# Segment softmax of a graph layer on one core: node maxima by scans of the sorted edges, exponentials per edge, sums with a bf16 one-hot

## The chip, the cores and the metric

One core of a Trainium2 chip runs the whole layer in one launch. The metric is the device time of that core in microseconds; lower is better. Three undisturbed runs of the kernel before took 2481.23, 2489.24 and 2489.09 us, median 2489.09 us.

## The reference

A graph attention layer over N = 12500 nodes with D = 64 features and E = 212500 edges that are sorted by target node (`dst`).

```python
h_trans = features @ Watt_w.T + Watt_b
e_raw = jnp.sum(h_trans[dst] * jnp.tanh(h_trans[src] + e_r), axis=-1, keepdims=True)
e_ij = leaky_relu(e_raw / 8)
max_score = segment_max(e_ij, dst, num_segments=N)
exp_e = jnp.exp(e_ij - max_score[dst])
denom = segment_sum(exp_e, dst, num_segments=N)
alpha = exp_e / (denom[dst] + 1e-09)
h_neigh = segment_sum(features[src] * alpha, dst, num_segments=N)
h_out = leaky_relu((features + h_neigh) @ W1_w.T + W1_b + ((features * h_neigh) @ W2_w.T + W2_b))
return layernorm(features + h_out)
```

## The kernel before

The nodes are cut into 98 **blocks** of 128. Since the edges are sorted, the edges of a block lie in one window of 19 tiles of 128 edges, and a step works on such a window. 16 tiles are laid out with 16 consecutive edges to a partition (MAIN), the last 3 (TAIL) with one edge of a tile to a partition. The tiles of a block are handled in five **chunks** of 4, 4, 4, 4 and 3.

A setup of some 60 us projects all nodes (h_trans) and writes a table in HBM with a node's projection and its features, 128 numbers to a row. Then each block passes through these stages:

- **Gathers.** GpSimd (POOL) issues one indirect DMA for each tile, 128 rows of 512 bytes into `got` (L528). 17 are always issued, the last two only where the window has edges there; there are 1716 in all. `got` has four buffers, so a gather may run up to four blocks ahead.
- **One-hot.** VectorE (DVE) builds `other` = (node of the block differs from the edge's target), 128x2432 in bf16 (L1055). TensorE (PE) transposes its 19 tiles (L778), ScalarE (ACT) turns them over into `hotT` (L624).
- **Scores.** PE spreads the target's projection to the edges with `hotT` in three bf16 parts (L793, 57 matmuls of 64 columns). DVE adds the gathered projection to the edge's attributes (L1066), ACT takes tanh (L630), DVE multiplies and sums (L1077, one instruction pair for each tile).
- **Maxima.** `finish_scores` on DVE splits the scores in three bf16 parts (six chained small instructions), PE transposes them (L801), ACT copies (L647), PE adds for each tile a mask matmul and a selection matmul (L813, L814), which lay all the block's scores out node by edge. DVE takes their maxima (L1098), splits the maximum in three parts (`split_max`, six chained small instructions), PE spreads it back to the edges (L821), DVE subtracts (L1117, L1119).
- **Weights.** ACT computes for each tile the whole 128x128 matrix of exp(mask + score - max) in float32 (L641, 19 of them).
- **Sums.** PE multiplies that float32 matrix with the gathered features and a column of ones (L833, 19 matmuls of 65 columns, which the trace records as two each).
- **Node part.** DVE divides (`neighbours`), PE transposes and multiplies with W1 and W2 (L839, L844), DVE adds, and takes the norm's statistics (`residual`).

The order on each engine is written out by hand in `step(third, before, prev, b, nxt, ahead)`. In one step block b is scored, b-1 (`prev`) gets its maxima, b-2 (`before`) its weights, sums and division, b-3 (`third`) its node part, and the one-hot of b+1 (`nxt`) is made; SyncE (SP) loads the edges of b and the indices of b+2. Each engine runs its list in order, and semaphores count blocks. Four steps stand ahead of a loop of 23 turns of four steps; two steps and a hand-written ending follow it. At the end, when 93 blocks have their statistics, DVE inverts the deviations (L1154), POOL normalises those blocks in four large instructions (L348, L350), and SP stores them; DVE normalises the last ones.

## Time and profile before

| what | value |
|---|---|
| median of the runs | 2489.09 us |
| span of the profiled execution | 3764.5 us |
| TensorE clock granted, mean of the span | 0.509 |
| busy PE / DVE / ACT / POOL in the span | 2446.1 / 1444.2 / 1070.6 / 1834.0 us |
| instructions PE / DVE / ACT / POOL | 17304 / 7626 / 3100 / 1744 |
| largest group | L528, the gathers on POOL: 1716 of 1047 ns |
| chain that ended last | another core or an unknown queue 33%, PE 31%, issue 16%, DVE 14%, ACT 4% |

The profiled execution took half as long again as the undisturbed runs, and it is the only one of which single instructions are known. So durations of instructions are read from it, while its waits have to be judged one by one. A matmul's end is modelled; how fast matmuls follow each other is read from their starts. "remote" is idle time for which the trace names no instruction as releaser. In the timeline a row gives start, duration, engine, line, operation, and in brackets the idle time ahead of it and what ended it.

### The profile page before, as it was taken

To read this page: it belongs to the slowest core of one execution; us is meant where nothing else is said; L and a number is where in the kernel's file an instruction comes from. 1 tells how busy PE (TensorE), PEld (TensorE's weight loads), DVE (VectorE), ACT (ScalarE), POOL (GpSimd) and SP (SyncE) were. 2 spreads that over 40 slices of the span, in tenths; PEclk is the share of its full clock that TensorE was granted. 3 is DMA by queue.
4 is the path that set the end of the run, shared out by engine and by line. 5 is a ranking of instruction groups with operands and counts; after the bars stand their busy time and mean duration, and the time that the engine had idled before them with its cause. 6 is when DMAs were issued, how large, how long until landed. Compare 5 with 4: busy or idle time off the path is not lost.

```text
span 3764.5 us, 55969 instructions
## 1 busy us (share of the span) xinstructions
PE 2446.1 (65%) x17304; PEld 1825.6 (48%) x17304; DVE 1444.2 (38%) x7626; ACT 1070.6 (28%) x3100; POOL 1834.0 (49%) x1744
## 2 busy tenths in 40 slices
PE   3367676767666666666676766667675757676666
PEld 2245454545454444545454545545454545455445
DVE  4234333333333333433343333434333433334335
ACT  3122222222323232323222232323222222223233
POOL 4554454545454545454544545454545444454542
PEclk7555555555555555555555555555555555555555
DMA  6111212121111121111112111111212111211111
GB/s 152 48 51 48 52 45 52 45 51 47 49 48 49 47 49 48 49 49 49 49 49 52 45 49 47 49 48 48 55 44 53 44 51 46 51 47 49 47 48 35
DMA packets 254023, 191.31 MB, mean 51 GB/s; under 512 B 201156, under 2 KB 213656, under 8 KB 253880
## 3 DMA queue, kind: packets, MB, share of 16 engines
q0 software_dynamic: 55072, 113.24, 11.5%
q1 hardware_dynamic: 198808, 76.77, 8.7%
q14 instruction: 128, 1.05, 0.1%
q8 instruction: 15, 0.25, 0.0%
HBM read 180.27 MB, written 9.60 MB: 50 GB/s over the span
## 4 chain that ended last, share of the span: by engine, by line
another core or an unknown queue 33%; PE 31%; issue 16%; DVE 14%; ACT 4%; SPq 1%; DMA 0%; POOL 0%; DVEq 0%; POOLq 0%
PE ps_sc L814 10%; PE ps_sc L813 9%; PE ps_acc L833 7%; DVE edge L1077 3%; ACT hotT L624 3%; PE ps_hd L793 2%; DVE chunk_max L1098 2%; PE ps_other L778 1%; DVE edge L1066 1%; PE ps_acc L844 1%; PE ps_acc L801 1%; DVE score L1092 1%; DVE score L1090 1%; DVE rest L1089 1%
## 5 line engine op out<-in xcount | busy, mean ns | idle before, releaser
L528 POOL DMA_INDIRECT got<-table,src_i x1716 | 1796.4, 1047 | 1821.1 <-issue 1800.6
L833 PE MATMUL ps_acc<-got,weight 128*128 128x65 f32 x3724 | 895.2, 422 | 4.3 <-issue 3.6
L778 PE MATMUL ps_other<-ident,other 128*128 128x128 bf16 x1862 | 289.6, 305 | 862.4 <-issue 627.7
L833 PEld LDWEIGHTS ps_acc<-got,weight 128*128 128x128 f32 x3724 | 828.2, 329 | 27.0 <-issue 3.1
L624 ACT ACTIVATE hotT<-ps_other 128x512 bf16<-128x512 bf16 (+1 forms) x490 | 274.2, 576 | 1395.1 <-remote 1232.7
L778 PEld LDWEIGHTS ps_other<-ident,other 128*128 128x128 bf16 x1862 | 186.0, 139 | 959.5 <-issue 687.4
L1098 DVE TENSOR_REDUCE chunk_max<-ps_sc 128x1 f32<-128x512 f32 (+1 forms) x490 | 325.9, 665 | 678.3 <-PE ps_sc L814 550.7
L641 ACT ACTIVATE weight<-other,arg 128x128 f32<-128x128 bf16 x1862 | 580.6, 387 | 8.4 <-DVE arg L1119 8.2
L793 PE MATMUL ps_hd<-h,hotT 128*128 (+1 forms) x5586 | 439.6, 240 | 196.7 <-issue 194.9
L813 PE MATMUL ps_sc<-mask,other 128*128 128x128 bf16 x1862 | 541.5, 291 | 26.9 <-ACT score3T L647 26.9
L814 PE MATMUL ps_sc<-score3T,sel 57*128 57x128 bf16 x1862 | 530.6, 285 | 0.0
L630 ACT ACTIVATE edge<-edge 128x256 f32<-128x256 f32 (+1 forms) x490 | 198.0, 404 | 1096.2 <-DVE edge L1066 1066.9
L1077 DVE CUSTOM_DVE_ANT_0 edge<-edge,ps_hd 128x64 f32<-128x64 f32 x1862 | 298.0, 216 | 501.1 <-remote 489.3
L793 PEld LDWEIGHTS ps_hd<-h,hotT 128*128 128x128 bf16 x5586 | 360.4, 131 | 258.9 <-issue 236.2
L813 PEld LDWEIGHTS ps_sc<-mask,other 128*128 128x128 bf16 x1862 | 226.1, 121 | 209.8 <-ACT score3T L647 27.6
L814 PEld LDWEIGHTS ps_sc<-score3T,sel 57*128 57x128 bf16 x1862 | 189.0, 101 | 233.9 <-issue 38.0
L1117 DVE TENSOR_REDUCE edge_max<-ps_misc 128x19 f32<-128x57 f32 x98 | 21.2, 217 | 717.5 <-remote 714.7
L1066 DVE TENSOR_TENSOR edge<-edge,got 128x256 f32<-128x256 f32 (+1 forms) x490 | 199.8, 408 | 9.7 <-DMA got<-table,src_i 7.6
L801 PE MATMUL ps_acc<-ident,score 128*57 128x128 bf16 x98 | 27.3, 279 | 195.0 <-DVE score L1092 170.9
L1077 DVE DVE_READ_ACCUMULATOR2_ANT raw<- 128x1 f32 x1862 | 153.9, 83 | 0.0
L1055 DVE TENSOR_TENSOR other<-iota_h,dst_rel 128x2432 bf16<-128x2432 bf16 x98 | 139.7, 1425 | 3.4
L801 PEld LDWEIGHTS ps_acc<-ident,score 128*57 128x57 bf16 x98 | 12.2, 125 | 207.8 <-issue 207.8
(116 smaller groups left out, 1061.1 us busy)
## 6 DMA issues: line engine op xcount, KB each, us to landing
edge<-in_edge_attr SPq DMA_DIRECT2D x98, 512.0 KB
got<-table,src_i POOLq DMA_INDIRECT x1716
edge<-in_edge_attr SPq DMA_DIRECT2D x98, 96.0 KB
table<-hx SPq DMA_DIRECT2D x12, 512.0 KB
got<-in_x SPq DMA_DIRECT2D x3, 768.0 KB, 14.3
src_i<-in_src SPq DMA_DIRECT2D x98, 8.0 KB
src_i<-in_src SPq DMA_DIRECT2D x98, 1.5 KB
dst_i<-in_dst SPq DMA_DIRECT2D x98, 8.0 KB
```

The source lines that it names most:

```text
L528: pool.indirect_dma_start(got[b.four][:, g, 0:2 * D], None, table, bass.IndirectOffsetOnAxis(ap=src_i[b.four][:, g:g + 1], axis=0), bounds ...
L624: act.activation(hotT[b.four][:, a:z, :], ps, ACT.Copy, bias=1.0, scale=-1.0)\
L630: act.activation(edge[b.two][:, a:z, :], edge[b.two][:, a:z, :], ACT.Tanh).then_inc(tanh_done[c], 1)
L641: last = act.activation(weight[:, g, :], other[b.four][:, g, :], ACT.Exp, bias=arg[b.two][:, g:g + 1], scale=-MASKED)
L778: last = pe.transpose(ps_other[(b.two + c) % 2][:, k * P:(k + 1) * P], other[b.four][:, g, :], ident16[:, :])
L793: last = pe.matmul(ps_hd[(b.two + c) % 2][:, k * D:(k + 1) * D], hotT[b.four][:, g, :], rhs, start=(part == 0), stop=(part == 2))
L813: pe.matmul(spread, other[b.four][:, g, :], mask16[:, :], start=True, stop=False)
L814: last = pe.matmul(spread, sel[:, g, :], score3T[:, :], start=False, stop=True)
L833: last = pe.matmul(a_sum, weight[:, g, :], got[b.four][:, g, D:2 * D + 1], start=(g == 0), stop=(g == TILES - 1))
L1066: dve.tensor_tensor(edge[b.two][:, a:z, :], edge[b.two][:, a:z, :], got[b.four][:, a:z, 0:D], ALU.add).then_inc(added[c], 1)
L1077: last = dve.tensor_tensor_reduce(out=edge[b.two][:, g, :], in0=edge[b.two][:, g, :], in1=ps_hd[(b.two + c) % 2][:, k * D:(k + 1) * D], sc ...
L1098: dve.tensor_reduce(chunk_max[:, c:c + 1], ps_sc[(b.two + c) % 2][:, 0:(z - a) * P], AX.X, ALU.max)\
```

## The change

- **Layout.** MAIN becomes 17 tiles and TAIL 2, still 19.
- **One-hot.** DVE builds `hot` (equal, not differing) in five chunks (L1074). PE transposes it and ACT copies it in three **pieces** of 8, 8 and 3 tiles. `hotT` has two buffers in place of four.
- **Maxima.** The split of the scores, their transposition and spreading, the maxima over node rows, the split and spreading of the maximum all go. In place of them: two scans on DVE along each partition's 17 edges, forwards and backwards, in which the difference of neighbouring target numbers times 2^100 resets the running maximum (`gap`); the first and last value of each partition and the two tail tiles are laid in one row of 512 on one partition by four PE transposes (`lay_rows`); two scans along this row (`scan_row`); four small PE transposes back (`lay_back`); and three instructions that combine (`exponents`). ACT prepares the target numbers (`set_ids`, five instructions), DVE their differences (`set_gaps`), SP loads the row of target numbers (`load_row`, two more DMAs).
- **Weights.** One exponential of 128x19 on ACT.
- **Sums.** DVE multiplies the gathered features with the weights (`weight_rows`, `rows`), ACT and DVE split them in turns in three bf16 parts (`split`, `rest`, into `triple`), and PE takes 19 bf16 matmuls of 195 columns with `hot`. DVE adds the three parts (L1163). All this is done one step earlier than before: the weights belong to `prev`. 
- **Ending.** The loop's step also serves for the ends. The large normalisation on POOL now starts after the last block's node part.

```diff
             def gather(third, before, prev, b, nxt, ahead):
-                    pool.wait_ge(summed[0], b.n - (BUFS - 1))
+                    pool.wait_ge(weighted[0], b.n - (BUFS - 1))
...
+            def weigh(b):
+                act.wait_ge(arg_done, b.n + 1)
+                act.activation(weight[:, :], arg[:, :], ACT.Exp).then_inc(weights_done, 1)
...
+            def lay_back(b):
+                for k in range(2):
+                    pe.transpose(m_back[:, k:k + 1], row_max[0:1, k:2 * P:2], ident[0:1, 0:1])
+                for k in range(TAIL):
+                    last = pe.transpose(m_back[:, 2 + k:3 + k], row_max[0:1, (2 + k) * P:(3 + k) * P], ident[0:1, 0:1])
...
+            def sum_edges(b, p):
+                pe.wait_ge(parts_done[p], b.n + 1)
+                for g in range(*piece(p)):
+                    last = pe.matmul(a_sum, hot[b.four][:, g, :], triple[:, g, 0:SUMS],
+                                     start=(g == 0), stop=(g == TILES - 1))
...
+                chain("fwd", dve.tensor_tensor_scan(run_max[:, :], gap[:, 0:MAIN], score[:, 0:MAIN], LOWEST,
+                                                    ALU.add, ALU.max), b)
+                ends = MAIN - 1
+                dve.tensor_tensor_scan(part_max[:, ends::-1], gap[:, MAIN:0:-1], run_max[:, ends::-1], LOWEST,
+                                       ALU.add, ALU.max).then_inc(runs_done, 1)
+            def scan_row(b):
+                dve.wait_ge(rows_ps, b.n + 1)
+                chain("row", dve.tensor_tensor_scan(row_max[:, :], row_gap[:, 0:ROW], ps_row[0:1, 0:ROW], LOWEST,
+                                                    ALU.add, ALU.max), b)
+                dve.tensor_tensor_scan(row_max[:, ROW - 1::-1], row_gap[:, ROW:0:-1], row_max[:, ROW - 1::-1], LOWEST,
+                                       ALU.add, ALU.max).then_inc(row_done, 1)
...
+            def weight_rows(b, p):
+                dve.tensor_tensor(rows[:, a:z, :], got[b.four][:, a:z, D:2 * D + 1],
+                                  weight[:, a:z].rearrange("p (g d) -> p g d", d=1).to_broadcast([P, z - a, D + 1]),
+                                  ALU.mult).then_inc(weighted[p], 1)
+            def rest(b, k, p):
+                    dve.tensor_tensor(rows[:, a:z, :], rows[:, a:z, :], parts[:, a:z, 0, :], ALU.subtract)\
...
+                    dve.tensor_tensor(parts[:, a:z, 2, :], rows[:, a:z, :], parts[:, a:z, 1, :], ALU.subtract)\
```

What stands on DVE in the middle of a step of the kernel before, from the second chunk of scores to the weights' arguments, in the last steps ahead of the loop:

```order
L1098 TENSOR_REDUCE chunk_max<-ps_sc0 128x1
L1104 TENSOR_REDUCE node_max<-chunk_max 128x1
L1105 CAST max3<-node_max 128x1
L1106 TENSOR_TENSOR mrest1<-node_max,max3 128x1
L1107 CAST max3<-mrest1 128x1
L1108 TENSOR_TENSOR mrest2<-mrest1,max3 128x1
L1109 CAST max3<-mrest2 128x1
L1050 TENSOR_SCALAR dst_rel<-dst_i0,base 128x38
L1053 TENSOR_SCALAR base<-base 128x1
L1055 TENSOR_TENSOR other0<-iota_h,dst_rel 128x2432
L1077 ISA edge1,raw1<-edge1,ps_hd1 128x64
```

And on DVE in a step of the changed kernel, in the loop, from the row scans to the first remainder:

```order
L1116 SCALAR_TENSOR_TENSOR row_max<-row_gap,ps_row 1x512
L1118 SCALAR_TENSOR_TENSOR row_max<-row_gap,row_max 1x512
L1085 TENSOR_TENSOR edge<-edge,got 128x256
...
L1074 TENSOR_TENSOR hot<-iota_h,dst_rel 128x512 x2
L1074 TENSOR_TENSOR hot<-iota_h,dst_rel 128x384
L1124 SCALAR_TENSOR_TENSOR first_max<-from_first,ps_misc,part_max 128x17
...
L1144 TENSOR_TENSOR rows<-got,weight 128x520 x2
L1144 TENSOR_TENSOR rows<-got,weight 128x195
L1085 TENSOR_TENSOR edge<-edge,got 128x256
L1153 TENSOR_TENSOR rows<-rows,triple 128x520 x2
```

The maxima's last link in split_max has gone, the one large one-hot has become short ones, and large elementwise work on the gathered rows has come to DVE (six of 520 and three of 195 numbers to a partition in a step).

On PE the changed kernel's step reads as follows (loop; the whole step is here, ahead of it stand the two rows of `dense` and expansion of the first piece):

```order
L832 MATMUL ps_hd1<-h3,hotT1 128x64 x24
L832 MATMUL ps_hd2<-h3,hotT1 128x64 x9
L858 MATMUL ps_misc<-ident,row_max 128x1 x2
L860 MATMUL ps_misc<-ident,row_max 128x1 x2
L870 MATMUL ps_acc<-triple,hot1 128x195 x19
L818 MATMUL ps_hot0<-ident16,hot0 128x128 x8
L818 MATMUL ps_hot1<-ident16,hot0 128x128 x8
```

The sums of the block before the last stand ahead of the transposes of the next block's one-hot, and on ACT the copy of the first of these pieces stands ahead of the exponential:

```order
L663 ACTIVATE edge<-edge 128x256 x2
L653 REGISTER_ALU
L658 ACTIVATE hotT<-ps_hot 128x1024
L683 ACTIVATE weight<-arg 128x19
L663 ACTIVATE edge<-edge 128x256
```

So the weights of a block now wait in line behind the sums, the transposes and a copy of other blocks.

## Rows read from the trace of the kernel before

**Rows 1.** The core: span, mean granted TensorE clock.
```profile
core 0: 3764.5 us, clock 0.509
```

**Rows 2.** Groups by form: count, busy us, mean ns, idle before.
```profile
L528 POOL DMA_INDIRECT got<-table,src_i x1716 | 1796.4, 1047 | 1821.1 <-issue 1800.6 <-remote 20.5
L1098 DVE TENSOR_REDUCE chunk_max<-ps_sc 128x1 f32<-128x512 f32 x392 | 271.2, 692 | 500.2 <-PE ps_sc L814 500.2
L1055 DVE TENSOR_TENSOR other<-iota_h,dst_rel 128x2432 bf16<-128x2432 bf16 x98 | 139.7, 1425 | 3.4
L1066 DVE TENSOR_TENSOR edge<-edge,got 128x256 f32<-128x256 f32 x392 | 164.5, 420 | 9.7 <-DMA got<-table,src_i 7.6
L624 ACT ACTIVATE hotT<-ps_other 128x512 bf16<-128x512 bf16 x392 | 232.6, 598 | 1384.0 <-remote 1223.4 <-issue 151.0 <-PE ps_other L778 7.3
```

**Rows 3.** Timeline, POOL, first gathers: start us, us, engine, line, [idle before].
```profile
58.11 1.17 POOL L528 DMA_INDIRECT got<-table,src_i  x1 [21.31 <-issue]
...
149.17 1.01 POOL L528 DMA_INDIRECT got<-table,src_i  x1 [0.30 <-issue]
180.53 1.00 POOL L528 DMA_INDIRECT got<-table,src_i  x1 [30.35 <-issue]
```

**Rows 4.** Timeline of DVE in the same stretch: a dot product waits.
```profile
129.91 0.22 DVE L1077 CUSTOM_DVE_ANT_0 edge<-edge,ps_hd 128x64 f32<-128x64 f32 x1 [30.85 <-remote]
...
130.06 0.22 DVE L1077 CUSTOM_DVE_ANT_0 edge<-edge,ps_hd 128x64 f32<-128x64 f32 x1
```

**Rows 5.** Timeline of POOL, three single gathers.
```profile
530.68 1.03 POOL L528 DMA_INDIRECT got<-table,src_i  x1 [0.30 <-issue]
...
905.56 1.17 POOL L528 DMA_INDIRECT got<-table,src_i  x1 [0.30 <-issue]
...
2009.39 1.74 POOL L528 DMA_INDIRECT got<-table,src_i  x1 [0.30 <-issue]
```

**Rows 6.** Timeline of DVE, what ran across the starts of those three gathers.
```profile
530.61 0.22 DVE L1130 TENSOR_TENSOR sum_prod<-h_neigh,hx 128x64 f32<-128x64 f32 x1 [0.16 <-issue]
530.75 0.22 DVE L1131 TENSOR_TENSOR sum_prod<-h_neigh,hx 128x64 f32<-128x64 f32 x1
...
905.49 0.35 DVE L1066 TENSOR_TENSOR edge<-edge,got 128x192 f32<-128x192 f32 x1
...
2008.82 1.43 DVE L1055 TENSOR_TENSOR other<-iota_h,dst_rel 128x2432 bf16<-128x2432 bf16 x1
```

**Rows 7.** Timeline of PE, merged runs: start us, us, count last.
```profile
2002.96 0.29 PE L813 MATMUL ps_sc<-mask,other 128*128 128x128 bf16 x1
2003.18 0.29 PE L814 MATMUL ps_sc<-score3T,sel 57*128 57x128 bf16 x1
...
2006.50 0.82 PE L793 MATMUL ps_hd<-h,hotT 128*128 x12
...
2007.13 3.66 PE L833 MATMUL ps_acc<-got,weight 128*128 128x65 f32 x16
...
2012.45 0.82 PE L778 MATMUL ps_other<-ident,other 128*128 128x128 bf16 x5
```

**Rows 8.** Timeline of DVE in the last steps, after the last gather.
```profile
3657.54 0.23 DVE L1137 TENSOR_TENSOR z<-ps_acc,b 128x64 f32<-128x64 f32 x1 [0.87 <-PE ps_acc L844]
...
3681.32 0.23 DVE L1137 TENSOR_TENSOR z<-ps_acc,b 128x64 f32<-128x64 f32 x1 [0.30 <-PE ps_acc L844]
...
3683.76 0.42 DVE L1066 TENSOR_TENSOR edge<-edge,got 128x256 f32<-128x256 f32 x1
...
3706.75 0.23 DVE L1137 TENSOR_TENSOR z<-ps_acc,b 128x64 f32<-128x64 f32 x1
```

**Rows 9.** Windows: stretch, PE, PEld, DVE, ACT, POOL busy, clock, DMA share, GB/s.
```profile
3660.00:3706.00 46.00, 41.70 (x307) 31.83 (x304) 24.02 (x138) 20.11 (x56) 0.00 (x0) 0.57 0.00 1
...
3717.00:3728.00 11.00, 0.02 (x1) 0.05 (x1) 10.86 (x6) 0.00 (x0) 10.71 (x3) 0.50 0.60 137
```

**Rows 10.** Timeline of POOL at the end.
```profile
3706.86 5.15 POOL L348 TENSOR_TENSOR hx<-hx,stats 128x2944 f32<-128x2944 f32 x1 [52.53 <-DVE rstd L1154]
```

More of the change, by code:

```diff
@@ L191, in gnn_layer @@
                    .rearrange("p (b d) -> p b d", d=D) for t in got]
-        hrest = [[other[2 + j][:, 8 * k:8 * (k + 1), :].rearrange("p g n -> p (g n)").bitcast(F32) for k in range(2)]
+        hrest = [[hot[2 + j][:, 8 * k:8 * (k + 1), :].rearrange("p g n -> p (g n)").bitcast(F32) for k in range(2)]
                  for j in range(2)]
@@ L286, in gnn_layer @@
         own = {name: sem(f"dve_{name}") for name in
-               ("rel", "base", "score", "s0", "r1", "s1", "r2", "nmax", "m0", "q1", "m1", "q2",
-                "emax", "den", "rden", "z1", "z2", "y", "bn", "aggr")}
+               ("rel", "base", "score", "fwd", "bwd", "row", "gap", "first", "last",
+                "sum", "den", "rden", "z1", "z2", "y", "bn", "aggr")}
         g_lower_set, g_fresh = scored[0], scored[1]
@@ L321, in pipeline @@
                     turn(t, k)
-            for k in range(TURNS * BUFS, BLOCKS):
+            for k in range(TURNS * BUFS, BLOCKS + 3):
                 turn(0, k)
@@ L817, in spread_max @@
-            def spread_max(b):
-                pe.wait_ge(max_split, b.n + 1)
-                for g in range(TILES):
-                    last = pe.matmul(m_max[:, 3 * g:3 * g + 3], hotT[b.four][:, g, :], max3[:, :],
-                                     start=True, stop=True)
-                last.then_inc(max_ps, 1)
-            def sum_edges(b, chunks):
-                for c in chunks:
-                    if c == 0 and follows(b, 1):
-                        pe.wait_ge(own["z1"], b.n)
-                    pe.wait_ge(weights_done[c], b.n + 1)
-                    for g in CHUNKS[c]:
-                        last = pe.matmul(a_sum, weight[:, g, :], got[b.four][:, g, D:2 * D + 1],
-                                         start=(g == 0), stop=(g == TILES - 1))
-                    last.then_inc(summed[c], 1)
+                last.then_inc(hd_ready[p], 1)
@@ L837, in transpose_sum_prod @@
+            def sum_edges(b, p):
+                if p == 0 and follows(b, 1):
+                    pe.wait_ge(own["z1"], b.n)
+                pe.wait_ge(parts_done[p], b.n + 1)
+                for g in range(*piece(p)):
+                    last = pe.matmul(a_sum, hot[b.four][:, g, :], triple[:, g, 0:SUMS],
+                                     start=(g == 0), stop=(g == TILES - 1))
+                if p == NP - 1:
+                    last.then_inc(summed, 1)
             def transpose_sum_prod(b):
```

536 lines of the change are left out of this document (270 added, 266 removed).

## The prediction

> **What bounds the kernel now.** I read the page first, then the groups by line and form, the timelines of POOL, DVE and PE in three places, and the windows.
>
> The profiled execution spans 3764.5 us at a mean granted clock of 0.509, which is the 1.2 GHz level nearly throughout [rows 1]. The undisturbed runs took 2489.09 us. So the sum can't be made from the span. The reader is to see why: while POOL issues its first 70 gathers without a pause, from 58.11 to 149.17 us [rows 3], DVE waits 30.85 us in one go for a product of PE that the trace lists no reason for [rows 4]. Such "remote" waits are a third of the chain. They can't be part of an undisturbed run: 1716 gathers of 1.047 us with the gap of 0.30 us behind each [rows 2, 3, 5] take 2311 us, 93% of 2489 us, so there POOL gathers nearly all the time and the other engines must work beside it. I therefore take durations from the profiled execution and rebuild the undisturbed time from two limits.
>
> The first is POOL: (1.047 + 0.300) x 1716 / 98 = 23.59 us for each block. With the first gather at 58.1 us [rows 3], 98 x 23.59 = 2311.8, 2.5 us (an estimate, from the issue of the last gather to its product) and an ending of 58.4 us (3764.5 less 3706.1, where the last block's products end, the moment ahead of the last row of [rows 8]) this gives 2431 us.
>
> The second is the circle of PE, DVE and ACT within a step. After the last gather the steps run without a remote wait, and the node part of a step starts at 3657.54, 3681.32 and 3706.75: 23.78 and 25.43 us a step [rows 8]. PE is busy for 41.7 of 46 us there, at a mean clock of 0.57 [rows 9]. Block 0 is through at about 58 + 23.6 + 2 = 83 us, so 2489 = 83 + 97 x P + 58.4 gives P = 24.2 us. That lies between the two steps seen, and 0.6 us above POOL's limit. So the circle, mostly PE at 1.2 GHz, most likely sets the time, and POOL stands close behind it. This is the fact that matters: whatever the change takes from PE, the gain ends at 23.6 us a step.
>
> **The change part by part.**
>
> POOL. The gathers stay: same number, same size. Their wait moves from the sums of block b-4 to its weighted rows, a step earlier, which only gives POOL more room. But what DVE does meanwhile changes. A gather that lasts 1.01 us at rest (the 149.17 row of [rows 3]) lasted 1.74 us when the one-hot's 1.43 us instruction ran across its start, and 1.17 when an addition of 0.35 us did [rows 5, 6]. In both cases the gather is held until some 0.12 us ahead of that instruction's end: 2010.25 - 0.12 - 2009.39 = 0.74, and 905.84 - 0.12 - 905.56 = 0.16. Both DVE instructions read two SBUF tensors. The Trainium skill says the same in the GPSIMD Engine Reference, section Specifications: GpSimd's SBUF interfaces are shared with VectorE, with contention when a VectorE instruction has two SBUF inputs or a 2-port mode; the trace agrees. An instruction of length d that falls anywhere in a gather's 1.35 us then costs on the average (d - 0.17)^2 / 2.7 us. For before: 0.59 for the one-hot and five times 0.02 for the additions, 0.69 us a block; measured are (1.047 - 1.010) x 17.5 = 0.65. The formula holds.
>
> After: a number costs DVE (0.420 - 0.361) / 64 = 0.92 ns when it adds (the 256 form [rows 2] against the 192 form, 0.35 to 0.36 [rows 6]), so 520 numbers take 0.6 to 0.66 us and 195 take 0.36. Six of 0.6 cost 0.07 each, 0.41 us; three of 0.36, 0.04; five one-hot chunks of 1.425 x 512 / 2432 + 0.06 = 0.36 us, 0.06; the additions 0.10; the row of gaps, 511 numbers, 0.07; the second row scan (two SBUF tensors, 1.1 us, below) 0.32 to 0.36. Sum 1.04 against 0.65, so **POOL's limit rises from 23.59 to 23.98 us**. Bounds: with row scans of 0.69 us it is 23.7. If POOL got no turn between instructions that DVE runs one right behind the other, three stretches of 1.45 us would cost 0.6 each, and the limit were 25.4. Against this speaks the gather at 530.68: two such instructions follow each other, and it was held 0.02 us, by the first one alone (530.83 - 0.12 - 530.68 = 0.03; the second would have made it 0.17) [rows 5, 6].
>
> PE. 38 matmuls of mask and selection at 0.22 us from start to start go (8.4 us), the float32 sums at 3.66 / 16 = 0.23 us a record, 38 of them, go (8.7 us) [rows 7], the spreading of the maximum and the transposed scores go (about 1 us). In come 19 bf16 matmuls of 195 columns. Their price has no row: 64 columns take 0.82 us for 12, about 0.055 each, so a column costs 0.85 ns and 195 of them 0.165; the mask matmuls took twice their 128 columns' worth, 0.22 for 0.11, an extra 0.11 [rows 7]. So 0.165 to 0.28 each, 3.4 to 5.3 us. I take the lower end, since transposes with a new weight for each matmul (L778) also run at (0.82 - 0.30) / 4 = 0.13 us for 128 columns [rows 7]. With eight small transposes (2 to 3 us) PE falls from some 21 us to 12 or 13. PE then hardly limits by its work, only by its place in the circle.
>
> DVE. Out: five maxima of 0.56 to 0.69 us, 3.3 us [rows 2]; the one-hot, 1.4; thirteen small instructions at (3683.76 - 3681.32) / 14 = 0.17 [rows 8], 2.3. In: one-hot chunks 1.6; nine passes over the rows, 6 x 0.57 + 3 x 0.3 = 4.3 from start to start; two row scans; the gaps 0.7; eight small ones, 1.5. A scan has no row. Below it stands a 512 maximum of 0.69 us, above it the 1.43 us of [rows 2]; I take 1.1. The Trainium skill's page "DVE: opcode table, instruction layouts, handler registers and perf-mode slots", section Datapath and trigger behaviour, says that this scan runs at half throughput. By it the 512 numbers would cost an estimated 1.1 to 1.2 us; by the maximum's rate, 0.69. The sum of a step differs by 0.9 us, and stays below POOL's limit either way. DVE's work goes from 14 us a step to 17 or 18.
>
> The circle. From the start of a DVE step:
> (a) residual, score, two short scans: 11 small ones, 1.9; an addition 0.35; place 0.4; two one-hot chunks 0.7; two row scans with their hand-over 2.4. Together 5.8 to 6.1.
> (b) Then the weights: four tiny transposes 1.1; the 19 sums of the block before the last, 3.4; eight transposes of the next one-hot 1.2; ACT's copy of 1024 numbers, 1.0 (twice the 512 form's 0.598 [rows 2], less its fixed part); the exponential 0.25; hand-overs 0.3. Together 7.2. DVE does a dot product, three one-hot chunks, the three combining instructions, an addition and a dot product in this time, some 3.4 us, and then stands idle for about 3.
> (c) ACT: tanh 0.35, two copies 1.35, the first split 0.65, hand-over 0.1: 2.5, over DVE's weighting of the rows.
> (d) DVE to the end: first remainders 1.5, 11 dot products at 0.15 [rows 4] 1.7, an addition 0.3, neighbours 1.4, second remainders 1.5, gaps 0.8: 7.2.
> 6.0 + 7.2 + 2.5 + 7.2 = **22.9 us**. Low end 21.5 (scans at 0.69, hand-overs overlapped), high end 24.9 (sums at 0.28 us).
>
> 22.9 is below 23.98, so POOL sets the pace and the circle's gain over 24.2 is cut off there.
>
> Start and ending. The setup up to the first gather loses only two POOL instructions on a table; POOL waits for the table of rows until 58 us anyway, so nothing. The ending: before, POOL's normalisation (four instructions of about 5.2 us [rows 10]) ran beside the last block. Now the last block's node part ends about 21 us after its products, and POOL's 21 us and the second half's store, 11 us (0.60 DMA share, 137 GB/s [rows 9]), come after, 2 to 3 us of the rest behind: 56 us against 58.4. If the last block needed 26, 61.
>
> **Sum:** 58.1 + 98 x 23.98 + 2.5 + 56 = 2466.7, I say **2467 us**, 0.9% below the median. What a measurement of this kernel can tell from no change is about 0.5%, 2476.6 to 2501.5.
>
> **The rivals.**
> Slower, the circle stays the bound. The place is (b): the weights of a block wait in line behind the sums, the transposes and a copy. If a 195-column matmul costs 0.28 us as the mask matmuls suggest, and the hand-overs that I put at 0.3 in all cost 1 us (the handing of scores from DVE over PE to ACT looks no faster), the step takes 25 us: 83 + 97 x 25.0 + 56 = 2564. It decides once (b) takes over 8.3 us instead of 7.2. For it: such hand sums leave things out. Against: the durations are all of this trace.
> Slower, POOL was already the bound, with 0.6 us a block of its own that the profile hides under its pauses (the loop's branches, the skipped tiles). Then 23.98 + 0.6 = 24.58: 2525. Against: between the first 70 gathers, across four blocks, every gap is 0.30 us.
> Faster: the gathers' 0.30 us gap belongs to the profiled execution, and POOL is quicker undisturbed. Then the circle's 22.9 bounds: 83 + 97 x 22.9 + 56 = 2360. Against: nothing else on POOL or DVE shows stretching.
> No change: POOL has the hidden 0.6 us, and the new DVE work doesn't hold it more than the old: 2489.
>
> **How the numbers follow.** Forecast (own range 2450 to 2485) 0.40; the circle slower 0.20; POOL with its hidden part 0.13; faster 0.15; no change 0.12. Faster by over 0.5%: 0.34 of the forecast's 0.40, and 0.15: 0.49. Within 0.5%: 0.06 and 0.12: 0.18. Slower 0.33. The range leaves out the greater part of the faster rival (0.10) and the upper half of the first one (0.10): 2390 to 2560.
>
> **What would show it.** Right: gathers of a mean of 1.07 us, most held ones across passes over the rows; DVE in the after profile some 17 us a step with one pause ahead of the first weighting; start-to-start of the 195-column matmuls near 0.165 us; row scans near 1.1 us. Wrong: POOL with pauses in the undisturbed pace, to be seen only if the steps after the last gather are longer than 24 us; a mean gather above 1.13 us; an addition that waits for a gather less than POOL's limit explains. Since the stretched waits come beside PE's many instructions, the span after should shrink far more than the time.

## The result, and the profile after

The changed kernel takes 2509.13 us (median of 4 runs, 2508.12 to 2513.11), the kernel before 2488.39 us beside it: a ratio of 1.0083, 95% interval 1.0062 to 1.0104. It is slower, by a little. The prediction was 2467 us, faster; the time lies inside its range, the direction is wrong.

The profile of the changed kernel: the page's head, its busy shares, its POOL row in 40 slices, and its chain by engine.

```profile
span 2506.4 us, 42957 instructions
PE 1062.9 (42%) x10542; PEld 914.5 (36%) x10542; DVE 1803.9 (72%) x8215; ACT 879.5 (35%) x2120; POOL 1896.3 (76%) x1741
...
POOL 2777777777777777777777777777777777777773
...
POOL 64%; issue 25%; POOLq 8%; SPq 1%; DMA 1%; DVE 1%; PE 0%; ACT 0%; DVEq 0%; ACTq 0%
```

This span is within 3 us of the time, so this profile can be read as it stands, which that of before could not [rows 1]. Its groups that answer to [rows 2] and [rows 6] (line, engine, operation, tiles, shapes, count, then busy time and mean ns of one, then the idle time ahead and what ended it):

```profile
L560 POOL DMA_INDIRECT got<-table,src_i x1716 | 1865.7, 1087 | 551.0 <-issue 551.0
L1085 DVE TENSOR_TENSOR edge<-edge,got 128x256 f32<-128x256 f32 x392 | 167.1, 426 | 369.4 <-DMA got<-table,src_i 367.0
L1074 DVE TENSOR_TENSOR hot<-iota_h,dst_rel 128x512 bf16<-128x512 bf16 x392 | 149.0, 419 | 3.4
L1144 DVE TENSOR_TENSOR rows<-got,weight 128x520 f32<-128x520 f32 x196 | 128.1, 694 | 76.4 <-ACT weight L683 76.3
L1118 DVE TENSOR_TENSOR_SCAN row_max<-row_gap,row_max 1x512 f32<-1x512 f32 x98 | 119.2, 1216 | 3.4
L1116 DVE TENSOR_TENSOR_SCAN row_max<-row_gap,ps_row 1x512 f32<-1x512 f32 x98 | 117.7, 1201 | 0.0
L1136 DVE TENSOR_TENSOR row_gap<-row_here 1x511 f32<-1x511 f32 x98 | 65.9, 672 | 0.0
```

Read it from POOL. The first gather starts at 58.18 us and the last ends at 2446.57, and in POOL's timeline every one of the 1715 gaps between them is 0.29 to 0.32 us. POOL never waits for anybody. The gathers themselves last 1.087 us on the average, against 1.01 at rest. The other engines wait for POOL: DVE's longest waits are those of the addition, L1085, for gathered rows, 376.5 us in 193 times. So POOL alone sets the time of the changed kernel, (2446.57 - 58.18 + 0.3) / 98 = 24.37 us a block. After the last gather come 59.8 us.

What a held gather looks like stands in POOL's timeline (start, length), and under it DVE's in the same stretch:

```profile
1507.82 1.03 POOL L560 DMA_INDIRECT got<-table,src_i  x1 [0.30 <-issue]
1509.15 1.58 POOL L560 DMA_INDIRECT got<-table,src_i  x1 [0.30 <-issue]
1511.04 1.01 POOL L560 DMA_INDIRECT got<-table,src_i  x1 [0.30 <-issue]
```

```profile
1508.84 1.01 DVE L1074 TENSOR_TENSOR hot<-iota_h,dst_rel 128x512 bf16<-128x512 bf16 x3
1513.58 0.43 DVE L1085 TENSOR_TENSOR edge<-edge,got 128x256 f32<-128x256 f32 x1 [3.02 <-DMA got<-table,src_i]
```

The gather of 1509.15 met three one-hot chunks in a row and was held 0.57 us, until 0.12 us ahead of the end of the last (1509.85 - 0.12 - 1509.15 = 0.58). About 30% of the gathers are held, for 133 us in all.

### The profile page after: what moved, and what is told of

Read it like the earlier page. It is cut to its first block, busy times and chain, and to the rows that moved or that the text cites. A ratio compares the mean times of both kernels' runs of the same rounds, so it can differ in the third digit from the quotient of the medians.

```text
span 2506.4 us, 42957 instructions
## 1 busy us (share of the span) xinstructions
PE 1062.9 (42%) x10542; PEld 914.5 (36%) x10542; DVE 1803.9 (72%) x8215; ACT 879.5 (35%) x2120; POOL 1896.3 (76%) x1741
## 4 chain that ended last, share of the span: by engine, by line
POOL 64%; issue 25%; POOLq 8%; SPq 1%; DMA 1%; DVE 1%; PE 0%; ACT 0%; DVEq 0%; ACTq 0%
POOL got L560 63%; POOLq L571 4%; POOLq L560 2%; POOLq L550 2%; SPq L422 1%; DMA triple<-in_dst 0%; POOL hx L374 0%; POOLq L568 0%; PE ps_acc L870 0%; POOLq L88 0%; POOL hx L376 0%; POOL hx L524 0%; POOLq L557 0%; DMA got<-table,src_i 0%; DMA dst_i<-in_dst 0%
## 5 line engine op out<-in xcount | busy, mean ns | idle before, releaser
L560 POOL DMA_INDIRECT got<-table,src_i x1716 | 1865.7, 1087 | 551.0 <-issue 551.0
L1085 DVE TENSOR_TENSOR edge<-edge,got 128x256 f32<-128x256 f32 (+1 forms) x490 | 201.8, 412 | 380.2 <-DMA got<-table,src_i 376.5
L658 ACT ACTIVATE hotT<-ps_hot 128x1024 bf16<-128x1024 bf16 (+1 forms) x294 | 236.5, 840 | 348.3 <-PE ps_hot L818 348.3
L870 PE MATMUL ps_acc<-triple,hot 128*128 128x195 bf16 x1862 | 301.6, 352 | 0.3 <-DVE z L1179 0.3
L695 ACT ACTIVATE triple<-rows 128x520 bf16<-128x520 f32 (+1 forms) x588 | 285.1, 549 | 16.9 <-DVE rows L1153 13.9
L870 PEld LDWEIGHTS ps_acc<-triple,hot 128*128 128x128 bf16 x1862 | 249.2, 140 | 19.2 <-DVE z L1179 0.5
L818 PE MATMUL ps_hot<-ident,hot 128*128 128x128 bf16 x1862 | 199.9, 280 | 73.1 <-ACT hotT L658 48.1
L1144 DVE TENSOR_TENSOR rows<-got,weight 128x520 f32<-128x520 f32 (+1 forms) x294 | 154.8, 581 | 76.4 <-ACT weight L683 76.3
L818 PEld LDWEIGHTS ps_hot<-ident,hot 128*128 128x128 bf16 x1862 | 174.7, 132 | 94.7 <-issue 67.3
L1074 DVE TENSOR_TENSOR hot<-iota_h,dst_rel 128x512 bf16<-128x512 bf16 (+1 forms) x490 | 175.3, 404 | 3.4
L1153 DVE TENSOR_TENSOR rows<-rows,triple 128x520 f32<-128x520 f32 (+1 forms) x294 | 154.3, 578 | 6.3 <-ACT triple L695 6.3
L1156 DVE TENSOR_TENSOR triple<-rows,triple 128x520 bf16<-128x520 f32 (+1 forms) x294 | 154.6, 581 | 0.0
```

The costliest lines, as they stand in the source:

```text
L560: pool.indirect_dma_start(got[b.four][:, g, 0:2 * D], None, table, bass.IndirectOffsetOnAxis(ap=src_i[b.four][:, g:g + 1], axis=0), bounds ...
L658: act.activation(hotT[b.two][:, a:z, :], ps, ACT.Copy).then_inc(hot_sb[p], 1)
L695: act.activation(parts[:, a:z, k, :], rows[:, a:z, :], ACT.Copy).then_inc(part_set[k][p], 1)
L818: last = pe.transpose(ps_hot[(b.two + p) % 2][:, k * P:(k + 1) * P], hot[b.four][:, g, :], ident16[:, :])
L870: last = pe.matmul(a_sum, hot[b.four][:, g, :], triple[:, g, 0:SUMS], start=(g == 0), stop=(g == TILES - 1))
L1074: dve.tensor_tensor(hot[b.four][:, a:z, :].rearrange("p g (n a) -> p g n a", a=2), iota_h[:, :].rearrange("p (z n a) -> p z n a", z=1, a=2 ...
```

## The experiments

"The kernel before" had two very different times in these runs: about 2490 us on the chips of the last three groups and of the result above, 3757 and 3762 us on those of the first two. The experiments that decide were made at 2490; the others stand at the end of this section.

**Controls.** Both kernels unchanged.

> The changed kernel as it is. It is the control of this call: the runs before it were made where the kernel before takes 3757 to 3762 us, and the changed kernel has no time of its own there. If the kernel before takes about 2489 us here: 2509, ratio 1.008, every gap between gathers 0.30. If it takes about 3760: the two neighbours took 3264 (forward row scan in PSUM) and 3414 (backward row scan twice), so 3270 to 3330, ratio 0.87 to 0.885, and the verdict on the change hangs on the condition in which it is timed. Rival: about 2510 in both conditions, since its profile shows no stall.

> The kernel before as it is, for its profile. If it takes about 2489 us here, its profile shows for the first time what bounds it undisturbed. Theory of the prediction: a circle of PE, DVE and ACT at 24.2 us a step, POOL pausing 0.6 us a block. Rival: POOL gathers without a pause (every gap 0.30) and its gathers are held for longer than the 0.65 us a block read in the stretched profile, about 1.2 us. If it takes about 3760 us: the same profile as at first, 3765 us.

Measured: after 2511.26 us, 1.0076 of before (1.0051 to 1.0101). Before 2492.78 us, and its profile, the first that is not stretched. Page and groups of before, in that run:

```profile
PE 2238.8 (90%) x17304; PEld 1781.2 (71%) x17304; DVE 1459.6 (59%) x7626; ACT 1070.6 (43%) x3100; POOL 1843.3 (74%) x1744
PE 82%; DVE 7%; issue 5%; POOL 3%; SPq 1%; DMA 1%; POOLq 0%; ACT 0%; DVEq 0%
L528 POOL DMA_INDIRECT got<-table,src_i x1716 | 1805.7, 1052 | 559.3 <-issue 548.4 <-PE ps_acc L833 11.0
```

PE is 82% of the chain and busy for 90% of the span. POOL's gathers last 1.052 us (1.047 in [rows 2]) and follow each other without a pause until 1625 us; from there on 14 gaps are longer, by 16 us together. The last ends at 2401.94, 92.5 us ahead of the end (59.8 in the changed kernel). So POOL runs ahead of the circle until its four buffers are full, and the circle sets the time, as the prediction had it, only that POOL's slack shows as a lead and not as a pause in each block.

**The two circles.** Six of the 17 to 19 gathers of a block are left out, in both kernels. Their chunks are still signalled, so the scores and sums of these tiles use old rows, and the outputs are not the layer's:

```diff
-                        if g < MAIN:
+                        if g in (0, 2, 4, 6, 8, 10):
+                            pool.inc_swdge_sem([gathered[b.four][c]], [16], mode="add")
+                        elif g < MAIN:
                             rows()
```

> The changed kernel without six of the main gathers in each block (the sums leave out these tiles' new rows). It leaves the circle of PE, DVE and ACT as the bound where the kernel before takes about 2489 us: the prediction's sum for it was 22.9 us a step, 2360 us. Rival (24.4 us a step, only just hidden behind POOL): 2500. It took 2522 and 2518 us where the kernel before took 3760.

> The kernel before without six of the main gathers in each block (the sums leave out these tiles' new rows). Its profile in the control shows PE on 82% of the chain and POOL without a pause but for 14 gaps, 16 us in all. Theory (the circle bounds, POOL stands close behind): 2475 to 2495. Rival (both bound it together, so that fewer gathers let DVE and PE go faster): 2440 to 2470. It took 3136 and 3138 us where the kernel before took 3760.

Measured: after 2260.55 us, 0.9061 of before (0.9038 to 0.9084); before 2476.39, 0.9909 (0.9878 to 0.9941), the lower edge of what the circle's theory allows. That is 18 us below the kernel before beside it (2494.55) and clear of noise, so the gathers are not quite free there; no run shows where these 18 us come from. By the prediction's own formula the circle of after is (2260.55 - 83 - 56) / 97 = 21.9 us a step, inside its 21.5 to 24.9 and quicker than the 22.9 taken. The circle of before is 24.1, for the 24.2 taken. In the changed kernel without the six gathers DVE no longer waits for data; it waits for the weights:

```profile
DVE rows L1146 <- ACT weight L685: 200.1, 96, 2.5
```

The starts of the backward row scan lie 21.92 us apart there on the average, which bears the 21.9 out. So the change did quicken the circle, by 2.2 us a step, 216 us between the two runs, and none of it reaches the time. The two kernels hang on different things: before on its circle with POOL 0.3 us a step behind it, after on POOL, which has become slower.

**Shorter passes, and a row scan in PSUM.** a_cut does the nine passes over the weighted rows (L1144, L1153, L1156) chunk by chunk; a_short has that, and the forward row scan in place in PSUM, so that the backward one reads one SBUF tensor:

```diff
+        ps_run = ps_row
-                chain("row", dve.tensor_tensor_scan(row_max[:, :], row_gap[:, 0:ROW], ps_row[0:1, 0:ROW], LOWEST,
+                chain("row", dve.tensor_tensor_scan(ps_run[0:1, 0:ROW], row_gap[:, 0:ROW], ps_row[0:1, 0:ROW], LOWEST,
-                dve.tensor_tensor_scan(row_max[:, ROW - 1::-1], row_gap[:, ROW:0:-1], row_max[:, ROW - 1::-1], LOWEST,
+                dve.tensor_tensor_scan(row_max[:, ROW - 1::-1], row_gap[:, ROW:0:-1], ps_run[0:1, ROW - 1::-1], LOWEST,
...
-                dve.tensor_tensor(rows[:, a:z, :], got[b.four][:, a:z, D:2 * D + 1],
+                for a, z in halves(p):
+                    last = dve.tensor_tensor(rows[:, a:z, :], got[b.four][:, a:z, D:2 * D + 1],
```

> The changed kernel with the row scan in PSUM (as in the first repeat) and with the nine passes over the weighted rows cut by chunk, 15 instructions of 260 or 130 numbers in place of nine of 520 or 195, each with two SBUF inputs but short. Theory of holding (a held gather loses what lies between its start and 0.12 us ahead of the end of the DVE instruction, so length counts squared): where the kernel before takes about 2489 us, 0.36 a block of the row scan go and of the 0.57 a block of the passes over 520 numbers (694 ns) about 0.35, 98 x 0.7 = 69 us, 2440 us, ratio 0.981. Rival (holding goes by the sum of DVE's time, not by the length of one): 2474. Where it takes about 3760: within 1% of the row scan's version, 3264.

> The changed kernel with the nine passes over the weighted rows cut by chunk into 15, and nothing else: the row scans and DVE's order are as in the changed kernel. The version with the row scan in PSUM beside the cut took 2482 us, 0.9956 of the kernel before, and its gathers were still held by what runs around the backward scan, 0.42 us a block. Theory (the cut alone gave that gain): 2475 to 2490 us, ratio 0.993 to 0.999. Rival (each needs the other): 2500 to 2511. The numbers are for a chip on which the kernel before takes about 2490 us.

Measured: a_short 2482.14 us, 0.9956 of before (0.9938 to 0.9974); it is the one version that is faster than both kernels. a_cut 2494.69 us, 1.0012 (0.9995 to 1.0029), 17 us below the changed kernel. A pass over 260 numbers takes 427 ns where 520 took 694. The two edits give 29 us, where the theory wanted 69; the cut alone gives 17, a little more than half of what was expected of it. One of the reasons stands in its trace: each hold counted to the DVE instruction that ran when the gather started, the passes fell from 0.62 us a block (control) to 0.25, but the backward scan rose from 0.40 to 0.51 and the additions from 0.14 to 0.19. The gathers that were let go met other instructions. The trace of a_short says why the row scan gave less: gathers that started inside the backward scan were still held. DVE and POOL there:

```profile
1057.47 1.21 DVE L1123 TENSOR_TENSOR_SCAN row_max<-row_gap,ps_row 1x512 f32<-1x512 f32 x1
1058.61 0.39 DVE L1090 TENSOR_TENSOR edge<-edge,got 128x256 f32<-128x256 f32 x1
```

```profile
1057.89 1.99 POOL L565 DMA_INDIRECT got<-table,src_i  x1 [0.30 <-issue]
```

The gather is held 0.98 us; the addition behind the scan ends at 1059.00, and 1059.00 - 0.12 - 1057.89 = 0.99. It is held to the end of the addition, that is also through a scan whose inputs are not both in SBUF. Of the gathers that started 0.2 to 0.7 us into this scan between 300 and 2300 us, 24 were held so and 13 not at all; among the 13 are all 6 behind which DVE had to wait for the rows that the addition needs. The semaphore records of the trace settle the other 7: for all 24 held gathers the last signal that the addition waits for had come before the gather started, for all 13 others it came after. So it is the addition, once it is ready, that holds.

**What stands behind the scan.** a_swap exchanges two calls of DVE's order; a_best has this and the cut, a_psswap all three edits:

```diff
                     scan_row(prev)
                 if exists(b):
-                    add(b, 1)
                     dot(b, 0)
+                    add(b, 1)
```

> The changed kernel with one exchange in DVE's order: the four dot products of the first chunk (one input in PSUM) stand behind the backward row scan, and the addition of the second chunk (two SBUF inputs) behind them instead of directly behind the scan. Every instruction stays as it is. New theory, read from the control's trace: no scan holds a gather itself; what holds it is the addition that stands next in line while the scan still runs (a gather that started 0.25 us after the scan's start was held 1.16 us, which is the end of the addition less 0.12 us; where the addition had to wait for its data, the same scan held nothing). With the exchange the 0.36 us a block go: 98 x 0.36 = 35 us, 2475 us, ratio to the kernel before 0.994. Rival (the backward scan itself holds, by its two SBUF inputs, as in the prediction): 2509. Rival (the hold just moves, since the addition now stands behind other work): 2500 to 2509. These numbers are for a chip on which the kernel before takes about 2489 us; where it takes 3760, within 1% of the changed kernel there.

> The exchange above, and the nine passes over the weighted rows cut by chunk into 15 instructions. The cut gave 29 us with a row scan in PSUM beside it that, by the new theory, gave nothing. The two together: 2509 - 35 - 34 = 2440 us, ratio 0.981, every gap between gathers 0.30. Rival (holding is not additive: gathers that are let go meet the next two-input instruction instead): 2460. Rival (the circle of PE, DVE and ACT becomes the bound at 24.2 us a step): 2480.

> The changed kernel with all three edits: forward row scan in place in PSUM, passes cut by chunk, and the dot products between the backward scan and the addition. Theory by the traces so far: the backward scan with one SBUF input holds no gather itself, and with the dot products behind it nothing that holds stands next in line, so a gather that starts within it lasts 1.01 to 1.02 us. Where the gathers then start against DVE's other instructions is open, since DVE waits for landings and keeps in step with the gathers: in the version with the exchange alone the gathers met the three one-hot chunks in a row, 0.57 us a block, and the time rose by 15 us. If they meet them here too: 2480 to 2500 us; if they fall as by chance, 0.36 us a block less than 2482: 2447. I take 2485.

Measured: a_swap 2525.88 us, 1.0121 of before (1.0099 to 1.0144), so 15 us slower where 35 faster were expected; a_best 2503.47, 1.0034 (1.0024 to 1.0045); a_psswap 2489.24, 0.9995 (0.9974 to 1.0015). The backward scan of a_swap, with two SBUF inputs and a dot product behind it:

```profile
1302.09 1.21 DVE L1118 TENSOR_TENSOR_SCAN row_max<-row_gap,row_max 1x512 f32<-1x512 f32 x1
1303.23 0.18 DVE L1096 CUSTOM_DVE_ANT_0 edge<-edge,ps_hd 128x64 f32<-128x64 f32 x1
1304.12 1.01 DVE L1074 TENSOR_TENSOR hot<-iota_h,dst_rel 128x512 bf16<-128x512 bf16 x3
```

```profile
1302.44 1.69 POOL L560 DMA_INDIRECT got<-table,src_i  x1 [0.30 <-issue]
1304.43 1.61 POOL L560 DMA_INDIRECT got<-table,src_i  x1 [0.30 <-issue]
```

and that of a_psswap, with one:

```profile
1261.25 1.21 DVE L1123 TENSOR_TENSOR_SCAN row_max<-row_gap,ps_row 1x512 f32<-1x512 f32 x1
1262.94 0.41 DVE L1090 TENSOR_TENSOR edge<-edge,got 128x256 f32<-128x256 f32 x1
1263.27 1.01 DVE L1079 TENSOR_TENSOR hot<-iota_h,dst_rel 128x512 bf16<-128x512 bf16 x3
```

```profile
1261.69 1.01 POOL L565 DMA_INDIRECT got<-table,src_i  x1 [0.30 <-issue]
1263.00 2.20 POOL L565 DMA_INDIRECT got<-table,src_i  x1 [0.30 <-issue]
```

The two-input scan holds a gather by itself: 0.68 us, to 0.18 us ahead of its end (1303.30 - 0.18 - 1302.44), and all 16 gathers that started 0.2 to 0.7 us into it between 300 and 2300 us were held; so the new theory of a_swap ("no scan holds itself") is refuted. The one-input scan holds none: of 83 gathers that started inside it between 300 and 2300 us, all lasted 1.01 us. So both halves are right: two SBUF inputs hold, and an instruction of that kind that stands next in line holds too, while a harmless one still runs. The Trainium skill's GPSIMD Engine Reference, section Specifications, names two SBUF inputs as a case of contention on the shared interfaces, and the traces agree; that the next instruction in line counts is shown by these traces alone.

Why did a_swap get slower all the same? The second gather of its fence was held 0.60 us by the one-hot chunks. It started 0.31 us into the first of the three, just as this one gave way, and had to wait for the third: 1305.13 - 0.12 - 1304.43 = 0.58. Between 300 and 2300 us this happened in 75 of 81 steps. It is nearly always the same place. In the changed kernel the next gather starts 0.9 us after the forward row scan in 60 of 82 steps of that stretch, while in the kernel before the starts against the one-hot, L1055, are spread over 0 to 1.3 us (the fullest tenth of a microsecond has 16 of 83). The likely reason is argued, not tested: DVE waits for landings of gathers in the changed kernel, so it starts its steps in step with them, and each gather of a block meets nearly the same instruction of DVE every time. Move one instruction, and the gathers meet others. a_swap took the hold around the scan from 0.37 to 0.14 us a block and raised that of the three chunks from 0.17 to 0.57. The exchange costs in all three pairs that differ by it alone: 15 us on the changed kernel, 9 beside the cut (a_cut to a_best), 7 beside both other edits (a_short to a_psswap). The scan in PSUM gives 13 us (a_cut to a_short) and 14 (a_best to a_psswap). The members of a pair ran on different chips, on which the kernel before differs by 1 to 4 us. The 14 us are not all that the scan held: in a_psswap it holds nothing, but the gathers that start in an addition or a one-hot are held for 0.88 us a block, against 0.35 in the control.

**A pause of POOL.** 16 waits that are always met behind each chunk.

```diff
+                    for _ in range(16):
+                        pool.wait_ge(consts, 11)
```

> The changed kernel with 16 waits of POOL that are always met after each chunk of four gathers, an idle of about half a microsecond to one (5 a block, 3 to 5 us a block). Theory (in the condition in which the kernel before takes about 3760 us, long rows of gathers one right behind the other starve PE and SP, and a pause of POOL lets them go on): the time falls clearly below the control's though POOL does more, below 3150. Rival (what starves them is the number of gathers, or a pause this short changes nothing): the same as the control or up to 98 x 4 = 390 us more. Where the kernel before takes about 2489 us, POOL's added time is seen in full: 2509 + 98 x 3 to 5, 2800 to 3000.

Measured: 2509.51 us, 1.0057 of before (1.0037 to 1.0078), the control's time. The 80 waits a block cost nothing and every gap stays 0.30 us, though the trace lists 3705 of the 7840 waits, seven or eight behind each chunk, some 0.6 us from the first to the last, partly while the next gather runs. So the gap between gathers is not time in which POOL's sequencer reads instructions, and what this run was made for, a pause where the others are starved, stays untested: this chip was not in that condition.

**The runs at 3757 us.** Here the kernel before takes 3757 us in the first group and 3762 in the second, in runs without a profile too, and its profile is that of [rows 1].

> The kernel before, but six of the 17 to 19 gathers of a block (tiles 0, 2, 4, 6, 8, 10) are left out: their semaphores are counted up without a transfer, so the scores and sums of these tiles use old rows. POOL then needs some 11.5 x 1.35 = 15.5 us a block. Theory 1 (the circle of PE, DVE and ACT sets the time of the kernel before, 24.2 us a step): 2475 to 2495 us, hardly changed. Theory 2 (POOL's gathers set the time before too, with more holding than its own profiled execution shows): the circle is shorter and shows itself, below 2440 us.

> The changed kernel with the same six gathers of a block left out (same tiles, old rows used). It lays the circle of the changed kernel bare. The prediction's own count gives 22.9 us a step: 83 + 97 x 22.9 + 56 = 2360 us, less some us since block 0 is through sooner. If the circle were the true bound of the changed kernel, 2500 us or more.

> The changed kernel, in which the forward scan along the row writes its result into PSUM, in place, and the backward scan reads it there: one SBUF tensor input instead of two. Nothing else moves. In the profile after, gathers whose start lay in the backward scan were held for 0.36 us a block in all. Theory 1 (time is POOL's, and only instructions with two SBUF inputs hold it): 98 x 0.36 = 35 us less than the changed kernel's 2509, so 2474 us, below the kernel before. If the holding has nothing to do with where the operand lies (the scan's length alone counts): no change, 2509.

> The kernel before with its one 128x2432 one-hot instruction cut into five by chunk, as in the changed kernel. The holding of gathers by it falls from 0.61 us a block to under 0.2, DVE's work rises by 0.3 us a step. Theory 1 (circle-bound before): 2485 to 2515 us, no gain. Theory 2 (POOL-bound before): some 40 us less, 2445 to 2455.

> The changed kernel with the backward row scan done twice, the second time into a row of its own that nothing reads, both with two SBUF inputs. DVE works 1.2 us more in each block. Theory (POOL sets the time and DVE's two-input instructions hold it): where the kernel before takes about 2489 us, the second scan holds as much as the first, 98 x 0.36 = 35 us (up to 50, since the two stand back to back), 2545 to 2560 us, and every gap between gathers stays 0.30. Rival (the circle of PE, DVE and ACT sets the time): 1.2 us a block, 118 us, 2627. Rival (DVE is hidden and holds nothing): 2509. Where the kernel before takes about 3757 us: the change of the time says whether DVE's length is on the path there, at most 118 us.

Measured: b_skip 3136.13 us (0.8348, interval 0.8334 to 0.8362) and again 3138.11; a_skip 2521.66 (0.6716, 0.67 to 0.6732) and again 2518.43; a_rowps 3263.84 (0.8683, 0.8668 to 0.8698) and again 3267.9; b_split, the one-hot of before cut into its five chunks, 3523.94 (0.9376, 0.936 to 0.9391); a_dose, where the backward row scan is done a second time, 3414.44 (0.9093, 0.9068 to 0.9117), which is 147 us above the repeat of a_rowps beside it, more than the 118 us that were expected at most. None of their expectations for 2489 us could be judged. What they do show: where POOL's 588 gathers less are worth at most 588 x 1.35 = 790 us, they save 620 us of before and some 740 us of the changed kernel (2522 for the 3264 of a_rowps), though POOL is busy for only about half of the time there. While gathers run in a row, the other engines get little done: from 1500 to 1513 us of a_dose PE is busy for 2.8 of 13 us, ACT for 0.4, DVE for 5.5. PE and POOL in the same stretch:

```profile
1501.57 0.21 PE L833 MATMUL ps_hd<-h,hotT 128*128 x1 [1.19 <-issue]
1503.01 0.21 PE L833 MATMUL ps_hd<-h,hotT 128*128 x1 [1.23 <-issue]
1504.42 0.21 PE L833 MATMUL ps_hd<-h,hotT 128*128 x1 [1.20 <-issue]
...
1526.79 1.49 PE L833 MATMUL ps_hd<-h,hotT 128*128 x24
```

```profile
1502.29 1.01 POOL L561 DMA_INDIRECT got<-table,src_i  x1 [0.30 <-issue]
1503.61 1.01 POOL L561 DMA_INDIRECT got<-table,src_i  x1 [0.30 <-issue]
1504.92 1.01 POOL L561 DMA_INDIRECT got<-table,src_i  x1 [0.30 <-issue]
...
1513.66 1.01 POOL L561 DMA_INDIRECT got<-table,src_i  x1 [0.30 <-issue]
```

PE, waiting for nobody, issues one matmul for each gather, 1.4 us apart, instead of 24 in 1.49 us. Within 2 us of the end of POOL's last gather of the row (1513.66) it is back to full speed. The stretch of [rows 3, 4] looks like the same thing: 70 gathers one behind the other, and DVE waits 30.85 us for PE. In most rows of a_dose it begins 10 or 11 gathers after the row has begun, and the gathers themselves are as quick as ever. Why a chip is in this condition, and what starves PE in it, stays open; that the changed kernel gains much there (0.87 by its neighbour a_rowps) while it loses 0.8% elsewhere is measured only by that neighbour, since the changed kernel itself was not run there.

## Why the prediction was wrong

**The bound of before: right.** The "remote" waits were no part of the undisturbed run, the circle set the time at 24.2 us a step (24.1 measured without the six gathers), and POOL stood close behind it: 23.59 predicted, (1.052 + 0.305) x 17.51 = 23.76 in the control.

**The cut-off: right.** POOL sets the pace of the changed kernel, and the circle's gain is cut off there. The circle itself, 22.9, was 21.9. Its rows held: 19 matmuls of 195 columns take 3.29 us, 0.162 from start to start, the low end, so the first rival (the circle stays the bound) fell on its price, and the skipping runs show it far away. (That rival's own figures, 1.9 us more for the sums and 0.7 for the hand-overs, give 25.5 us a step and not 25.0.) The rival "faster", where the 0.30 us gap belongs to the profile, is out too: the span with the gap equals the time without a profile.

**The size of the holding: wrong, and this is the step that failed.** The sum took 1.04 us a block and found 1.35, the mean gather at 1.087 for the 1.07 named. The forecast for POOL's limit, 23.98, was 24.37, 98 x 0.39 = 38 us of the 42 between prediction and time (the rest is 1 us in the ending and 3 between the span and the median). By the prediction's own formula it splits in two.

- The durations. A pass over 520 numbers was put at 0.6 us and takes 0.694; the scan was put at 1.1 and takes 1.216; a one-hot chunk 0.36, in truth 0.419. The rate of 0.92 ns a number came from the pair 192 and 256, whose difference is 0.06 us and whose shapes differ little; from 195 to 520 numbers it is (694 - 354) / 325 = 1.05 ns. The holding goes by the square of the length less 0.17 us. (The prediction does not say why it takes off 0.17 where its two rows show 0.12; what fits is that in the changed kernel a gather that starts in the first 0.04 us of the backward scan is not held, 6 of 6.) With the measured lengths the prediction's own formula gives 0.65 for the passes (0.45 predicted), 0.41 for the backward scan (0.32 to 0.36), 0.10 for the one-hots (0.06), 0.11 for the additions (0.10), 0.09 for the gaps (0.07): 1.36 us, against the 1.35 found. So the mean gather, 1.0872 us for 1.0694, is 1716 x 0.0178 = 31 us of the 38, and by the formula it is all rounded and extrapolated durations.
- The gap, the other 8 us. It was read as 0.30 us and is (2446.57 - 58.18 - 1865.7) / 1715 = 0.3048: 1716 x 0.0048 = 8 us. The timeline prints two decimals, and some of the gaps are 0.31; the two ends of a row of gathers give the mean.

The trace bears out only the sum. Each hold counted to the DVE instruction that ran when the gather started, the changed kernel has 0.57 us a block for the passes, 0.39 for the backward scan, 0.21 for the one-hots, 0.15 for the additions and 0.01 for the gaps. Against the predicted terms the one-hots are the largest miss, 0.15 us, before the passes with 0.12, and the one-hots' lengths explain 0.04 of it: the rest is where the gathers fell. So the lengths were too short, that is measured; what share of the 31 us is theirs and what share the places', stays open.

The Trainium skill's page "DVE: opcode table, instruction layouts, handler registers and perf-mode slots", section Datapath and trigger behaviour, which says that this scan runs at half throughput, would have put it at an estimated 1.1 to 1.2 us. The trace agrees with 1.20 and 1.22.

**The rule of the holding: right in the mean, wrong in the single case.** The formula takes gathers as falling anywhere. In the kernel before they do, and it fits (0.69 by formula, 0.65 and, in the control, 0.72). In the changed kernel they don't, and its agreement there is partly luck, as the terms above show: of the two versions in which only DVE's order or nothing but lengths changed, a_swap went up by 15 us where the formula says no change or less, and a_cut went down by 17 where it says 32. The prediction also dismissed the case that several such instructions in a row give POOL no turn, by one gather that got its turn. Both occur: the 0.60 us of a_swap is a gather that missed its turn between the first and the second, 1.19 us in a_psswap one that waited for the end of four instructions (1264.28 - 0.12 - 1263.00 = 1.16).

**Start and ending: right.** First gather at 58.18 for 58.1, and 59.8 us behind the last gather for 58.5.

**The chances.** 0.33 stood on slower, for a circle that did not get quicker (0.20) and for a hidden part of POOL's own (0.13). Neither happened. What happened had no rival of its own: the forecast's mechanism with its long durations 11 to 16% longer, and gathers that do not fall by chance. A forecast of 0.9% that hangs on a term that goes by the square of unseen durations should have had its sizes varied, and "same" and "slower" fed from that. 520 numbers at 0.7 us, the scan at 1.2, would have given 1.29 us of holding, 24.2 us a block and 2491 us, no longer a forecast of faster.

## What to carry to other kernels

When a resource stands 2% behind the bound, an edit that relieves the bound is worth at most these 2%, so the price that the edit puts on that second resource must be worked out to the same accuracy as the gain. Take prices of unseen shapes from rows on both sides of them, vary each, and look what the sum does. Where POOL issues gathers without a pause, look at each long DVE instruction with two SBUF inputs, and at what is next in line behind long harmless ones: shorter instructions, or an input in PSUM, free it; an exchange in the order may make it worse, since the gathers can meet the same instruction in nearly every step. And compare a profile's span with the time measured before a word of it is used: here one belonged to another condition than the other.

## What the runs showed of the hardware that was not expected

- A gather waits at its start only, until 0.12 us ahead of the end of a DVE instruction with two SBUF inputs; of the 21 gathers of the changed kernel that started from 0.3 us ahead of a row of one-hots to 0.03 us into it, none was held. A backward scan of 1 x 512 with both inputs in SBUF held it (0.18 us ahead of its end), with one in PSUM it did not, in 83 of 83 cases.
- An instruction that holds, standing ready behind a scan that doesn't, holds from the scan's time on: 0.98 us in a_short for an addition of 0.39 us. What decides is whether its last signal came before the gather started, in all 37 cases 0.2 to 0.7 us into the scan.
- Gathers and DVE fall in step: the same place in 60 of 82 steps, and 75 of 81 in a_swap, so that the exchange of two calls costs 15 us.
- Sixteen met waits on POOL behind each chunk of gathers, some 0.6 us by the trace, cost nothing.
- The same kernel takes 2490 us in one condition and 3760 in another, and in the second PE issues one instruction for each gather, about 1.4 us apart, in most rows once ten or eleven gathers have followed each other.
